# A fused AdaLN attention and expert block: another order of the linear-attention stage, a PSUM bank of its own for states and outputs, feature runs of three

## The reference

```python
qkv = h @ W_attn + b_attn                      # 16 heads of 16
phi = exp(einsum('bhtd,dm->bhtm', x, omega) - 0.5 * sum(x * x)) / sqrt(128)
kv = phi_k[..., :, None] * v[..., None, :]
S, Z = cumsum(kv, axis=2), cumsum(phi_k, axis=2)
num = einsum('bhtm,bhtmd->bhtd', phi_q, S)
den = einsum('bhtm,bhtm->bht', phi_q, Z) + EPS
x = x + ga * ((num / den) @ W_proj + b_proj)
# then: layernorm, top 2 of 4 experts over relu(x Wi + lora) Wo, and x + gb * out
```

## Time and profile before

| | us |
|---|---|
| median of 3 runs | 826.2 |
| lowest, highest | 823.42, 828.61 |
| profiled execution | 827.64 |
| its span, first to last instruction | 825.9 |
| a loop block | 94.9 |

### The profile page before, as it was taken

The page is one execution under the profiler, slowest core; times in us unless marked ns, Lnnn a source line. Parts: engine busy times, 40 slices in busy tenths (PEclk is TensorE's granted clock), DMA queues, the critical chain, the costliest instruction groups (busy, mean ns, idle before and its releaser), DMA issues.

```text
span 825.9 us, 16957 instructions
## 1 busy us (share of the span) xinstructions
PE 766.3 (93%) x6138; PEld 605.5 (73%) x6138; DVE 547.2 (66%) x1289; ACT 409.9 (50%) x758; POOL 46.9 (6%) x62
## 2 busy tenths in 40 slices
PE   2989999999999999999999999999999999998696
PEld 2767767977688767977688766977679776886466
DVE  5546666776766766776766766776667767666356
ACT  2365544664366444654466545555446643663222
POOL 1101000010000100010000100010000100010000
PEclk9969999999999999999999999999999999999689
DMA  8680073202802064101722046020732028010000
GB/s 270 145 203 5 2 207 81 77 0 70 213 2 76 0 172 113 51 26 51 191 43 76 0 117 169 0 76 0 206 79 76 0 74 209 2 52 2 0 1 26
DMA packets 46540, 65.37 MB, mean 79 GB/s; under 512 B 8716, under 2 KB 22840, under 8 KB 46392
## 3 DMA queue, kind: packets, MB, share of 16 engines
q1 hardware_dynamic: 46520, 65.10, 29.4%
HBM read 39.87 MB, written 25.17 MB: 79 GB/s over the span
## 4 chain that ended last, share of the span: by engine, by line
PE 85%; DVE 9%; ACT 2%; issue 1%; SPq 1%; DMA 1%; DVEq 0%; POOL 0%; POOLq 0%; ACTq 0%
PE pa L514 11%; PE prod L529 7%; PE ring L493 6%; PE ring L380 6%; PE pa L380 5%; PE ring L381 4%; PE ring L382 4%; PE pa L382 4%; PE pa L381 4%; PE prod L548 4%; PE pa L620 4%; PE ring L498 3%; PE ring L643 2%; PE prod L514 2%; PE ring L696 2%; PE prod L538 2%
## 5 line engine op out<-in xcount | busy, mean ns | idle before, releaser
L514 PE MATMUL pa<-phq,phkT 128*128 128x128 f32 x896 | 115.6, 276 | 0.0
L514 PEld LDWEIGHTS pa<-phq,phkT 128*128 128x128 f32 x896 | 108.4, 192 | 2.4 <-issue 1.6
L821 ACT ACTIVATE phq<-ring 128x512 f32<-128x512 f32 x96 | 58.9, 614 | 91.3 <-PE ring L493 90.3
L1078 DVE TENSOR_TENSOR am_phk<-pa,const 128x512 f32<-128x512 f32 x112 | 74.3, 686 | 33.2 <-PE pa L514 33.2
L1231 DVE SCALAR_TENSOR_TENSOR am_phk<-ring,am_phk 128x512 f32<-128x512 f32 x64 | 44.3, 692 | 53.2 <-PE ring L696 53.2
L380 PE MATMUL pa<-wo_r,qk_r 128*128 128x256 f32 x256 | 72.1, 282 | 0.6 <-DVE qk_l L1236 0.6
L382 PE MATMUL pa<-wo_l,qk_r 128*128 128x256 f32 x256 | 72.2, 282 | 0.0
L883 ACT ACTIVATE qk_r<-phq 128x512 fp32r<-128x512 f32 x64 | 40.5, 632 | 63.7 <-DVE phq L1240 63.7
L381 PE MATMUL pa<-wo_r,qk_l 128*128 128x256 f32 x256 | 71.8, 281 | 0.0
L529 PE MATMUL prod<-am_phk,v_ones 128*32 128x256 f32 x1024 | 61.9, 382 | 4.6 <-DVE tg L1109 4.6
L380 PE MATMUL ring<-h_r,wi_r 128*128 128x512 f32 x128 | 57.9, 452 | 4.2 <-DVE am_phk L1231 3.6
(11 more groups left out here) (189 smaller groups left out, 1568.2 us busy)
## 6 DMA issues: line engine op xcount, KB each, us to landing
xq<-qk_parts SPq DMA_DIRECT2D x48, 512.0 KB
qk_parts<-qk_r SPq DMA_DIRECT2D x32, 256.0 KB, 3.6
qk_parts<-qk_l SPq DMA_DIRECT2D x32, 256.0 KB, 4.0
tok<-in_L_attn_x SPq DMA_DIRECT2D x8, 512.0 KB, 4.9
xr<-in_L_attn_x SPq DMA_DIRECT2D x8, 512.0 KB, 4.0
out_x<-tg SPq DMA_DIRECT2D x16, 256.0 KB, 2.2
norm_parts<-norm_r SPq DMA_DIRECT2D x16, 128.0 KB, 3.6
norm_parts<-norm_l SPq DMA_DIRECT2D x16, 128.0 KB, 5.1
```

What stands on the lines that cost most here:

```text
L514: mm = pe.matmul(score_bank(q, a)[:, tt], phkT[:, q % 2, a, tt], phq[:, q // 2 % 2, 2 * (q % 2) + a, tt], start=True, stop=True)
L821: act.activation(dst, src, ACT.Exp).then_inc(exp_done.sem, 1)
L1078: dve.tensor_tensor(am[:, 2 * (q % 2) + a, :].rearrange("p (c t) -> p c t", c=NT), score_bank(q, a)[:].rearrange("p (c t) -> p c t", c=NT) ...
```

## The change

- The transposed state contributions, the reads and the transposed outputs go to one bank of their own, `turn` (ring 3), instead of to `prod`. Features rotate over three ring banks. The last q/k projection goes to ring 1; the second half of y's transposes to a bank of `prod`.
- TensorE's list: state_reads(gr-1) and products(gr) stand next to each other, out_transpose(gr-1) behind them. Features go in two runs of three tiles. For pairs 4 to 7, scores(q, 0) stand behind the first run of their own pair and scores(q, 1) behind the second. products no longer wait for the division, state_transpose does. state_reads wait for the whole state at once. values wait for qk_split 4. transpose1 waits bank by bank for the last exponentials.
- ScalarE and VectorE follow that order; their two copies of the products wait for the add of the reads before. VectorE does `ln1_stats` in front of copy(0).

In the three `attend` functions below the removed lines are left out; they stand in the functions printed above.

```diff
@@ -59,6 +59,8 @@
...
+RUN = TILES // 2
+RING = 3
@@ -208,11 +210,13 @@
...
-        qk_bank = [pa[0], pa[1], ring[2], ring[3]]
+        turn = ring[RING][:].rearrange("p (c m) -> p c m", c=NT)
+        qk_bank = [pa[0], pa[1], ring[2], ring[1]]
+        y_bank = [ring[0][:], pb[0]]
...
-        proj_bank = lambda tile: pb[tile % 2] if tile < 2 * TILES else ring[tile % 4]
+        proj_bank = lambda tile: pb[tile % 2] if tile < 2 * TILES else ring[tile % RING]
@@ -406,9 +410,11 @@
...
-            def transpose1(n):
+            def transpose1(n, after=None):
                 wait(pe, hn_ready, n, NT)
                 for k in range(KT):
+                    if after is not None:
+                        wait(pe, exp_done, after, PAIRS * TILES - RING + k + 1)
                     for t in range(NT):
@@ -434,6 +440,7 @@
...
             def values(n):
+                wait(pe, qk_split, n, 4)
                 for t in range(NT):
@@ -487,8 +494,8 @@
...
                         wait(pe, exp_done, n, tile - 1)
-                    if tile >= 2 * TILES + 4:
-                        wait(pe, exp_done, n, tile - 3)
+                    if tile >= 2 * TILES + RING:
+                        wait(pe, exp_done, n, tile - RING + 1)
                     if k < 4:
@@ -519,8 +526,6 @@
...
                     wait(pe, v_done, n, 2)
-                else:
-                    wait(pe, y_step, n, 3 * gr)
                 wait(pe, am_done, n, GROUP * (gr + 1))
@@ -532,78 +537,82 @@
...
             def state_transpose(n, gr):
+                if gr:
+                    wait(pe, y_step, n, 3 * gr)
                 for c in range(NT):
...
                         wait(pe, copied[c // 2], n, gr + 1)
-                    mm = pe.transpose(prod[:, c, 1, :], prod_sb[:, c, 1, :], ident)
+                    mm = pe.transpose(turn[:, c, :], prod_sb[:, c, 1, :], ident)
                 mm.then_inc(d_ps.sem, 1)
             def state_reads(n, gr):
+                wait(pe, s_step, n, (NT + 1) * (gr + 1))
                 for c in range(NT):
-                    if c % 2 == 0:
-                        wait(pe, s_step, n, (NT + 1) * gr + c + 3)
                     for j in range(GROUP):
                         rows = slice(j * VA, (j + 1) * VA)
-                        mm = pe.matmul(prod[rows, c, 1, :], s_sb[:, c, rows], phq[:, gr % 2, j, c * P:(c + 1) * P],
+                        mm = pe.matmul(turn[rows, c, :], s_sb[:, c, rows], phq[:, gr % 2, j, c * P:(c + 1) * P],
                                        start=True, stop=True)
...
             def out_transpose(n, gr):
...
                 for c in range(NT):
-                    mm = pe.transpose(prod[:, c, 0, :], oT_sb[:, c, :], ident)
+                    mm = pe.transpose(turn[:, c, :], oT_sb[:, c, :], ident)
                 mm.then_inc(o_ps.sem, 1)
             def attend(n, front_next):
...
+                first, second = range(RUN), range(RUN, TILES)
                 scores(n, 0, 0)
                 scores(n, 0, 1)
...
+                features(n, 2, first)
                 scores(n, 1, 0)
...
+                features(n, 2, second)
                 scores(n, 1, 1)
...
+                features(n, 3, first)
+                products(n, 0)
+                features(n, 3, second)
+                scores(n, 2, 0)
+                state_transpose(n, 0)
+                scores(n, 2, 1)
+                scores(n, 3, 0)
+                scores(n, 3, 1)
+                for gr in range(1, GROUPS):
                     q = 2 * gr + 2
+                    state_reads(n, gr - 1)
                     products(n, gr)
...
+                    if q < PAIRS:
+                        features(n, q, first)
+                    out_transpose(n, gr - 1)
+                    if q < PAIRS:
                         scores(n, q, 0)
+                        features(n, q, second)
+                        scores(n, q, 1)
                     elif front_next:
                         qk(n + 1, 0, [0])
                         qk(n + 1, 1, [0])
                     state_transpose(n, gr)
...
+                    if q < PAIRS:
+                        features(n, q + 1, first)
                         scores(n, q + 1, 0)
+                        features(n, q + 1, second)
+                        scores(n, q + 1, 1)
+                        if front_next and gr == GROUPS - 2:
+                            transpose1(n + 1, n)
                     elif front_next:
                         qk(n + 1, 0, [1])
                         qk(n + 1, 1, [1])
                         qk(n + 1, 2, [0])
...
+                state_reads(n, GROUPS - 1)
+                if front_next:
+                    qk(n + 1, 2, [1])
+                out_transpose(n, GROUPS - 1)
...
                     for t in range(NT):
-                        mm = pe.transpose(ring[k][:, t * P:(t + 1) * P], y[:, t, k * P:(k + 1) * P], ident)
+                        mm = pe.transpose(y_bank[k][:, t * P:(t + 1) * P], y[:, t, k * P:(k + 1) * P], ident)
                     mm.then_inc(yT_ps.sem, 1)
@@ -821,26 +830,29 @@
...
             def attend(n, front_next):
...
+                def copy(gr):
                     wait(act, prod_ps, n, 2 * gr + 1)
+                    if gr:
+                        wait(act, oT_added, n, gr)
                     act.activation(prod_sb[:, 0:2].rearrange("p c k m -> p (c k m)"), pb[0],
                                    ACT.Copy).then_inc(copied[0].sem, 1)
...
+                features(n, 2, range(TILES))
+                features(n, 3, range(RUN))
+                copy(0)
+                features(n, 3, range(RUN, TILES))
+                for gr in range(1, GROUPS):
+                    copy(gr)
+                    if gr + 1 < GROUPS:
+                        features(n, 2 * gr + 2, range(TILES))
+                        features(n, 2 * gr + 3, range(TILES))
                     if front_next and gr == GROUPS - 2:
                         front_hT(n + 1)
...
                     wait(act, yT_ps, n, k + 1)
-                    act.activation(yT[:, k, :], ring[k][:], ACT.Copy).then_inc(yT_done.sem, 1)
+                    act.activation(yT[:, k, :], y_bank[k], ACT.Copy).then_inc(yT_done.sem, 1)
@@ -1091,17 +1103,17 @@
...
                     after = s_sb[:, c + 1, :] if c + 1 < NT else state[:, 1, gr, :]
-                    dve.tensor_tensor(after, s_sb[:, c, :], prod[:, c, 1, :], ALU.add).then_inc(s_step.sem, 1)
+                    dve.tensor_tensor(after, s_sb[:, c, :], turn[:, c, :], ALU.add).then_inc(s_step.sem, 1)
             def add_reads(n, gr):
                 wait(dve, read_ps, n, gr + 1)
-                dve.tensor_tensor(oT_sb[:], prod_sb[:, :, 0, :], prod[:, :, 1, :], ALU.add).then_inc(oT_added.sem, 1)
+                dve.tensor_tensor(oT_sb[:], prod_sb[:, :, 0, :], turn, ALU.add).then_inc(oT_added.sem, 1)
             def divide(n, gr):
...
                     wait(dve, out_done, n, out_done.per)
-                o = prod[:, :, 0, :].rearrange("p c (j d) -> p c j d", j=GROUP)
+                o = turn.rearrange("p c (j d) -> p c j d", j=GROUP)
                 dve.tensor_scalar(den[:], o[:, :, :, DH], EPS_DEN, None, ALU.add).then_inc(y_step.sem, 1)
@@ -1112,39 +1124,49 @@
...
             def attend(n, front_next):
+                def copy(gr):
+                    wait(dve, prod_ps, n, 2 * gr + 2)
+                    if gr:
+                        wait(dve, oT_added, n, gr)
+                    dve.tensor_copy(prod_sb[:, 2:4].rearrange("p c k m -> p (c k m)"), pb[1])\
+                        .then_inc(copied[1].sem, 1)
                 for q in range(2):
                     for a in range(2):
                         causal_scores(n, q, a)
...
+                if front_next:
+                    ln1_stats(n + 1, False)
+                copy(0)
+                causal_scores(n, 2, 0)
+                advance_state(n, 0)
+                causal_scores(n, 2, 1)
+                causal_scores(n, 3, 0)
+                causal_scores(n, 3, 1)
+                for gr in range(1, GROUPS):
                     more = gr + 1 < GROUPS
                     q = 2 * gr + 2
...
+                    add_reads(n, gr - 1)
+                    if front_next and not more:
+                        split_h(n + 1, hT_r, 2, hT_parts, [0])
+                    copy(gr)
+                    divide(n, gr - 1)
+                    if front_next and gr == 1:
+                        normalize_apply(n + 1, tok, ln1_pool, hn_ready)
                     if more:
                         causal_scores(n, q, 0)
+                        causal_scores(n, q, 1)
+                    elif front_next:
+                        split_h(n + 1, hT_r, 2, hT_parts, [1])
                     advance_state(n, gr)
                     if more:
...
                         causal_scores(n, q + 1, 0)
+                        causal_scores(n, q + 1, 1)
                     elif front_next:
                         split_qk(n + 1, 0)
...
```

(72 more changed lines are left out.)

10 lines of the change are left out of this document (removed).

## The result

The changed kernel takes 911.5 us (median of 4 runs, 908.4 to 918.2); the kernel before, run beside it, 825.0. The ratio is 1.105, with a 95% interval of 1.102 to 1.108. Forecast were 895 (864 to 928), and slower by over 1% with a chance of 0.92.

What follows compares the result with a forecast made beforehand. TensorE, busy 93%, was taken as the bound. Blocks 1 to 6: 3.5 + 1.85 + 4.4 + 1.95 - 2.1 = 9.6 us each; block 0 6.1, last 4.5; +68 on 827.6 gives 896, forecast 895 (864 to 928).

Steps and rivals of the forecast that it cites:

- Cost 1, scores behind their features: Groups 1 and 2, second half: TensorE's scores wait for ScalarE's exponentials, 2.2 us a group, 4.4 a block (3.6 to 5.2).
- Cost 2, the wait for copy(0): Group 0, blocks 1 to 6: statistics wait for the token load ahead of copy(0), so TensorE idles 3.5 us.
- Cost 2, the tie: Group 0: VectorE's state copy against GpSimd's addition; scores(3,1) wait 0.8 us or, GpSimd first, 2.9; middle 1.85 taken.
- Cost 3, the values: Values(n+1) wait for qk_split 4 and begin 2.25 us late; 1.95 us in seven blocks (1.5 to 2.25).
- The clock: Rival: idling around group 0's scores lowers TensorE's clock, 2 to 3.4 us a block, six times; 912 us, chance 0.22.
- Gains: Joined runs, no division wait before products(3), and no late state copy in group 1: together 2.1 us a block.
- The wait for the division: In front of products(3): the wait goes, since products and outputs no longer share a bank; gain 0.49 us.
- the late state copy of group 1: Copy beside GpSimd's addition takes 1.53 us, not 0.23, making reads late and slow; leaving group 1 gains 0.85.
- The joined run: Reads(gr-1) next to products(gr) save one exit from and entry to 32-column work: 0.25 us, three times a block, 0.75.
- The three-bank ring itself costs little: Feature tiles on three banks: at ScalarE's 0.5 us per tile, banks are free when the next run comes.

Runs made afterwards that it cites:

- The later order: The changed kernel with each half pair's scores of pairs 4 to 7 behind the next half's features: 880.1 us, 1.069.
- the last experiment: The kernel before, with only GpSimd's addition made to wait for the state steps of group 1: 817.4 us, 0.991.
- the first experiment: The changed kernel with ln1_stats back behind the first division and the normalization one group later: 879.2 us, 1.067.

## Why the prediction was right, and where it wasn't

**The sign and the mechanisms** were right, each cost taken out by itself: the statistics (32 us; put into the kernel before, 30), the scores behind their own features (31), the values wait (11). These undone together, with GpSimd's addition and one mask placed anew, give back the whole. The sizes were less good than the total, as follows.

**Cost 1, scores behind their features.** Predicted 0.5 + 0.4 + 0.9 + 0.4 a group. The 64 waits come to 25.8 us, 3.2 a block (0.78 and 0.29 for the odd pair above), and full-clock periods give 3.3 to 3.5. That is under the lower bound of 3.6 and 1.2 under the 4.4 taken. The later order gave back 3.9 a block by the medians, but those hold the clock as well.

**Cost 2, the wait for copy(0).** Predicted a landing 4.9 after issue and 3.5 idle; measured 4.95 and 18.0 us in six blocks, 3.0 each (2.7 to 3.2). The mechanism is right, the size 0.5 too large.

**Cost 2, the tie.** This term was mis-sized. "The rows cannot split a tie of 0.02 us, so I take the middle, 1.85": the prediction itself said that no block would lie there. GpSimd came first by 0.10 to 0.12 us in all of blocks 1 to 6, and at the full clock the scores waited 2.75 (end: 2.9). Moving the addition leaves 0.66 (other end: 0.8). With 2.9 in place of 1.85 the prediction's period is 10.65 longer than before; the shortest measured one is 105.95 - 94.9 = 11.05 longer. Both ends were priced well, and one of them should have been the sum, the other a rival. The copy was held until the addition's end, for as much of its 2.35 as was left. That agrees with the Trainium skill (SBUF — State Buffer, Who interferes with whom): who issues second is blocked for the other's whole instruction. No run shows VectorE's copy first in a close tie.

**Cost 3, the values.** Predicted 1.95, bounds 1.5 and 2.25; 1.8 in the kernel before and, by the estimate above, 1.95 in the changed one. Right.

**The clock.** A rival with a chance of 0.22, and it came, at the low end of its price. Six periods at 11.05 would be 66.3; they were 78.6 longer, so the clock took 12.3 us of the profiled execution, where 2 to 3.4 a block (12 to 20) had been set. The median of 911.5 all but equals this rival's 912, but the clock is little more than half of what the forecast lacked. Why it was dearer in one block than in another shows in the fourth block, where the half-clock scores lay ahead of a wait and cost nothing:
```profile
391.08 0.44 PE L545 MATMUL ring<-const,prod_sb 128*128 128x128 f32 x2 [3.18 <-DVE prod_sb L1131]
391.35 3.36 PE L521 MATMUL pa<-phq,phkT 128*128 128x128 f32 x16
...
396.07 1.16 PE L521 MATMUL pa<-phq,phkT 128*128 128x128 f32 x8 [1.36 <-DVE am_phk L1090]
```
Sixteen scores took 3.36 instead of 1.95, and the wait behind them 1.36 instead of 2.75. In the second block the stretch covered scores and reads behind the last wait, and there nothing swallowed it. In two blocks it lasted longer, 10.2 and 6.8 us. The argument held against this rival, that 1.18 busy of 2 us had left the clock alone at 212, was one sample: after a wait of 2.2 at the same place the clock fell in five of seven blocks of one experiment and in four of seven of another.

**Gains.** The wait for the division and the late state copy of group 1 did go. The late copy was worth more than 0.85, 0.97 in the kernel before, but the change doesn't gain it, it only moves the addition onto a worse copy. The joined run was priced 0.25 each and gave 0.17 to 0.19. "The three-bank ring itself costs little" is not borne out: with the costs undone, what remains of the change is 0.6 us a block slower than the order of before with the same wait on GpSimd. Of the 2.1 us a block only 94.92 - 94.57 = 0.35 came, and GpSimd's better place alone is worth more than that.

**The sum.** 896 on the profiled execution against 918.2, 22.4 more than the 895.8 before rounding: 6.3 for the tie (1.05 in each of six periods), 2.4 for the remaining 0.4 of the period, 12.3 for the clock, 1.0 behind the last y transposes, 0.8 ahead of the first (4.9 for 4.15) and -0.4 in the last period (6.05 for 6.45; the values wait of the last front is counted there). That the period came within 0.4 is partly luck. By the waits the four costs are 3.0 + 2.75 + 3.2 + 1.95 = 10.9, where the prediction with the right end of the tie had 12.75 less 2.1 of gains. Two costs were 1.7 too high, the gains were missing, and the errors nearly cancelled. By the medians it is 911.5 for 895; the profiled execution was the longest of the four, with a mean clock of 0.96 where the others had up to 0.969.

## What to carry to other kernels

When one instruction moves in a list that an engine takes in order, walk the list once for its own input (is it there yet?) and once for whoever it now stands in front of; here moving four statistics ahead of one copy cost more than everything the change could gain. A close tie between two engines for the same port is to be priced by its ends and not by its middle, and then forced: one wait that holds GpSimd's addition back until VectorE's state copy of group 1 is through made the kernel before 0.9% faster, the best result here. Price a saved change of form (narrow to full-width matmuls and back) against what pays for it: 0.17 us each is easily lost again. And where a sum comes out right, measure its terms too: here two errors cancelled.

## What the runs showed of the hardware

- TensorE's idling of 2.2 us at the values wait was followed, in five of seven blocks and not in the other two, by 3.4 us at 1.2 GHz (mean clock 0.57 over 218.5 to 222.5, 1.00 over 118 to 122). Such a stretch costs 1.5 us there, and in the one block where a wait lay behind it nothing. With the waits gone there are none in the loop, as in the kernel before. The Trainium skill (TensorE: Matmul & The Clock Gate, HAM oscillation) describes such recurring falls; the traces agree, but behind the values wait they don't come in every iteration.
- A VectorE copy of 128x128 that begins 0.12 us after GpSimd's 128x1024 addition lasts 2.32 us, to the addition's end, instead of 0.22; one that begins 0.36, 0.91 or 0.99 later lasts 2.08, 1.53 or 1.46, again to its end. In the last experiment a mask and the addition L1098 run beside GpSimd's and keep their times (1.28 for two masks, 1.27 in the earlier trace rows; 0.69): not every VectorE operation is held. Nor is every copy: in the last block of the first experiment VectorE's copy L1131 of the products began 0.06 behind the addition and kept its 0.69. All that kept their times take an operand from TensorE's results; the copy that is held takes none. The traces show no other operation without such an operand beside the addition.
